# Table rows of eight words, sums cleared by ScalarE, edge attributes copied late, loads of x awaited one later: a graph network on one core

## The reference, cut to what matters

```python
def sage_layer(x, src, dst, Wl, bl, Wr):                  # three of them, relu after the first two
    agg = segment_sum(x[src], dst, 6250)
    cnt = segment_sum(ones, dst, 6250)
    return (agg / clip(cnt, 1)) @ Wl + bl + x @ Wr

x = layernorm(x + sage(x))
z = concatenate([x[dst], x[src], edge_attr_16])           # 100000 x 272
msg = sigmoid(z @ Wf.T + bf) * softplus(z @ Ws.T + bs)
h = relu(layernorm(batchnorm(segment_sum(msg, dst, 6250)) + x))
out = layernorm(x + (h + x))
```

## Time and profile before

| | us |
|---|---|
| median of 3 runs | 3432.28 (3430.3 to 3433.51) |
| the profiled execution | 3432.11 |
| its span | 3430.4 |
| PE busy / DVE / ACT / POOL | 2659.0 / 2137.3 / 1224.4 / 2346.7 |
| mean granted TensorE clock | 0.911 of full speed |

### The profile page before, as it was taken

The page is one execution under the profiler, slowest core; times in us unless marked ns, Lnnn a source line. Parts: engine busy times, 40 slices in busy tenths (PEclk is TensorE's granted clock), DMA queues, the critical chain, the costliest instruction groups (busy, mean ns, idle before and its releaser), DMA issues.

```text
span 3430.4 us, 69755 instructions
## 1 busy us (share of the span) xinstructions
PE 2659.0 (78%) x16221; PEld 1989.6 (58%) x16222; DVE 2137.3 (62%) x4942; ACT 1224.4 (36%) x1682; POOL 2346.7 (68%) x2399
## 2 busy tenths in 40 slices
PE   6578888675887875757888856688888888888874
PEld 6345555574655555645655556556666666666654
DVE  6635445466432224566544556778888888888886
ACT  2423333011000000110000002267888888888866
POOL 3667777576777777767777777467777777776610
PEclk8789999897999997878998978999999999999997
DMA  5354444323655562237777643344444444444411
GB/s 156 100 189 148 130 148 130 96 74 105 174 158 143 148 160 51 73 102 230 235 239 220 195 115 109 90 138 126 127 125 127 126 127 126 126 117 117 115 52 38
DMA packets 346021, 454.93 MB, mean 133 GB/s; under 512 B 135643, under 2 KB 260599, under 8 KB 342311
## 3 DMA queue, kind: packets, MB, share of 16 engines
q0 software_dynamic: 88624, 207.58, 22.5%
q10 hardware_dynamic: 127520, 197.33, 18.0%
q1 hardware_dynamic: 129768, 48.71, 5.8%
HBM read 357.03 MB, written 101.90 MB: 134 GB/s over the span
## 4 chain that ended last, share of the span: by engine, by line
POOL 35%; PE 20%; issue 20%; DVE 10%; DMA 9%; DVEq 2%; SPq 2%; ACT 2%; POOLq 0%; ACTq 0%
POOL shared L762 26%; POOL shared L802 9%; DMA shared<-q_dram,idx 6%; PE ps L957 6%; PE ps L948 4%; PE ps L1188 3%; PE ps L940 2%; SPq L637 1%; DVE work L2377 1%; DVE work L2060 1%; PE ps L967 1%; DMA dense_dram<-work 1%; ACT work L1521 1%; PE ps L1207 1%; PE ps L1191 1%
## 5 line engine op out<-in xcount | busy, mean ns | idle before, releaser
L762 POOL DMA_INDIRECT shared<-y_even,idx x1056 | 1039.4, 984 | 399.0 <-issue 311.5
L802 POOL DMA_INDIRECT shared<-q_dram,idx x784 | 779.1, 994 | 282.3 <-issue 224.5
L948 PE MATMUL ps<-shared,work 128*128 x4368 | 665.2, 301 | 324.4 <-SPq L598 194.2
L948 PEld LDWEIGHTS ps<-shared,work 128*128 128x128 f32 x4368 | 605.6, 211 | 400.0 <-issue 388.6
L2087 DVE TENSOR_TENSOR acc<-acc,ps 128x129 f32 x546 | 155.3, 284 | 848.3 <-PE ps L948 654.4
L762 POOL DMA_INDIRECT shared<-y_odd,idx x528 | 511.1, 968 | 178.1 <-issue 159.7
L1188 PE MATMUL ps<-pq,work 128*128 x1664 | 502.1, 404 | 142.6 <-issue 96.9
L2377 DVE TENSOR_TENSOR work<-ps,shared 128x256 f32<-128x256 f32 x832 | 294.5, 416 | 174.5 <-PE ps L1191 148.7
L1188 PEld LDWEIGHTS ps<-pq,work 128*128 128x128 f32 x1664 | 259.3, 196 | 237.8 <-issue 167.8
L967 PE MATMUL ps<-pq,work 128*128 128x385 bf16 x1456 | 296.1, 354 | 61.2 <-DVE work L2074 24.2
L1375 ACT CAST work<-ps 128x600 bf16<-128x600 f32 x260 | 159.6, 662 | 340.7 <-PE ps L940 314.8
(11 more groups left out here) (368 smaller groups left out, 3883.0 us busy)
## 6 DMA issues: line engine op xcount, KB each, us to landing
work<-counts_dram ACTq DMA_DIRECT2D x156, 384.0 KB
counts_dram<-work ACTq DMA_DIRECT2D x26, 1568.0 KB
ea_parts<-work ACTq DMA_DIRECT2D x128, 196.0 KB
ea_sb<-ea_parts SPq DMA_DIRECT2D x196, 128.0 KB
work<-counts_dram ACTq DMA_DIRECT2D x52, 416.0 KB
shared<-y_even,idx POOLq DMA_INDIRECT x1056
shared<-q_dram,idx POOLq DMA_INDIRECT x784
shared<-y_odd,idx POOLq DMA_INDIRECT x528
```

The lines of the kernel that those rows point to most:

```text
L762: pool.indirect_dma_start(msg[:, u, 0:F], None, y_two[layer % 2], bass.IndirectOffsetOnAxis(ap=idx[:, u:u + 1], axis=0)).then_inc(s_quad[q ...
L802: pool.indirect_dma_start(q_ring[:, u * 2 * F:(u + 1) * 2 * F], None, q_dram, bass.IndirectOffsetOnAxis(ap=idx[:, u:u + 1], axis=0)).then_ ...
L948: last = te.matmul(ps[:, SUM_BANKS[i], 0:FA], lhsT=oh4[:, OH_SLOTS[i], u, :], rhs=shared[:, bass.ds(place + u * FA, FA)], start=u == 0, st ...
```

## The change

- In all row loads of PE, DVE and SP's convolution loop the second load takes four words instead of three; the register arrays have eight entries. The table DMAs fill all eight words of a row.
- POOL's loop that clears `acc` goes; ACT clears a chunk after it has normalized it and issued the load of x, the last chunk after the last copy of q.
- The copy of the attributes is cut in its two halves, issued by SP ahead of the last two turns of layer 1; SP's last turn but one is taken out of the loop in all layers.
- ACT waits for a load of x before it issues the next one, and no longer right behind its issue.

```diff
             for at_, row_, first_, turns_, n_, wide_ in Q_TABLES:
-                from_dram = bass.AP(..., [[NIC * P, 1], [n_, turns_], [1, n_]])
+                from_dram = bass.AP(..., [[NIC * P, 1], [n_, turns_], [1, wide_ if turns_ > 1 else n_]])
...
-            def copy_sorted():
+            def copy_attributes(h):
                 with sp.If(unsorted < 1):
-                    for h in range(2):
-                        sp.dma_start(eaT_sorted[:, h * EP // 2:(h + 1) * EP // 2],
-                                     eaT[:, h * EP // 2:(h + 1) * EP // 2]).then_inc(s["ea_sorted"], 16)
+                    sp.dma_start(eaT_sorted[:, h * EP // 2:(h + 1) * EP // 2],
+                                 eaT[:, h * EP // 2:(h + 1) * EP // 2]).then_inc(s["ea_sorted"], 16)
...
                 turn(0)
-                if not layer:
-                    copy_sorted()
-                with sp.Fori(1, QG // RQ - 1) as it:
+                with sp.Fori(1, QG // RQ - 2) as it:
                     turn(it)
-                turn(QG // RQ - 1)
+                for h in range(2):
+                    if not layer:
+                        copy_attributes(h)
+                    turn(QG // RQ - 2 + h)
...
-                    sp.reg_load(n_regs[k:k + 4], q_regs[0:1, bass.ds(m * WIDE + (CONV_DONE_AT - WIDE + k), min(4, RC - k))])
+                    sp.reg_load(n_regs[k:k + 4], q_regs[0:1, bass.ds(m * WIDE + (CONV_DONE_AT - WIDE + k), 4)])
...
-            with pool.Fori(0, NCH) as it:
-                pool.wait_ge(s["var_z"], it + 1)
-                gp.tensor_copy(acc[:, bass.ds(it * (CW * FA), CW * FA)], zero[:, :].to_broadcast([P, CW * FA]))\
-                    .then_inc(s["acc_clear"], 1)
...
-                        pe.reg_load(t_regs[k:k + 4], q_regs[0:1, bass.ds(it * WIDE + (NEEDED_AT + k), min(4, IT - k))])
+                        pe.reg_load(t_regs[k:k + 4], q_regs[0:1, bass.ds(it * WIDE + (NEEDED_AT + k), 4)])
...
             def load_x(c):
+                if c:
+                    act.wait_ge(s["x_in"], c * 16)
+                alone(act)
                 act.dma_start(y_again[c % 2], xv[:, c * CW:(c + 1) * CW, :]).then_inc(s["x_in"], 16)
-                act.wait_ge(s["x_in"], (c + 1) * 16)
...
+            def clear_sums(it):
+                sc.copy(acc[:, it * (CW * FA):(it + 1) * (CW * FA)], zero[:, :].to_broadcast([P, CW * FA])).then_inc(s["acc_clear"], 1)
...
                 norm_x1(it)
                 if it < 2:
                     next_x(NCH - 2 + it)
+                if it < NCH - 1:
+                    clear_sums(it)
                 copy_x1(it)
                 copy_q(it)
+            clear_sums(NCH - 1)
...
-                    dve.reg_load(a_regs[k:k + 4], q_regs[0:1, bass.ds(it * WIDE + (SUMS_AT + k), min(4, IT - k))])
+                    dve.reg_load(a_regs[k:k + 4], q_regs[0:1, bass.ds(it * WIDE + (SUMS_AT + k), 4)])
```

More of the change, by code:

```diff
@@ L550, in _ @@
             for at_, row_, first_, turns_, n_, wide_ in Q_TABLES:
-                from_dram = bass.AP(q_regs_dram.tensor, q_regs_dram.offset + row_ * NIC * P + first_, [[NIC * P, 1], [n_, turns_], [1, n_]])
-                sp.dma_start(q_regs[0:1, at_:at_ + turns_ * wide_].rearrange("o (t e) -> o t e", e=wide_)[:, :, 0:n_] if turns_ > 1
+                from_dram = bass.AP(q_regs_dram.tensor, q_regs_dram.offset + row_ * NIC * P + first_, [[NIC * P, 1], [n_, turns_], [1, wide_ if turns_ > 1 else n_]])
+                sp.dma_start(q_regs[0:1, at_:at_ + turns_ * wide_].rearrange("o (t e) -> o t e", e=wide_) if turns_ > 1
                              else q_regs[0:1, at_:at_ + n_].rearrange("o (t e) -> o t e", e=n_), from_dram).then_inc(s["tab_back"], 16)
@@ L600, in turn @@
                 def turn(it):
-                    n = RQ if not isinstance(it, int) or it == 0 else RQ - AHEAD
+                    n = RQ if not isinstance(it, int) or it < QG // RQ - 1 else RQ - AHEAD
                     first = it * RQ + SUMMED_AT
@@ L629, in _ @@
             sp.wait_ge(s["p_done"], (NCH - 1) * 4 + 4)
-            n_regs = [sp.alloc_register(f"sp_n{q}") for q in range(RC)]
+            n_regs = [sp.alloc_register(f"sp_n{q}") for q in range(WIDE)]
             done_regs = [sp.alloc_register(f"sp_d{q}") for q in range(RC)]
@@ L909, in _ @@
             pe.wait_ge(s["tab_back"], TAB_Q)
-            t_regs = [pe.alloc_register(f"pe_t{u}") for u in range(IT)]
-            g_regs = [pe.alloc_register(f"pe_s{u}") for u in range(IT)]
+            t_regs = [pe.alloc_register(f"pe_t{u}") for u in range(WIDE)]
+            g_regs = [pe.alloc_register(f"pe_s{u}") for u in range(WIDE)]
             q_needed = [pe.alloc_register(f"pe_q{u}") for u in range(IT)]
-            d_regs = [pe.alloc_register(f"pe_d{u}") for u in range(IT)]
+            d_regs = [pe.alloc_register(f"pe_d{u}") for u in range(WIDE)]
             def sage_sums(layer):
@@ L924, in load_turn @@
                     for k in range(0, IT, 4):
-                        pe.reg_load(t_regs[k:k + 4], q_regs[0:1, bass.ds(it * WIDE + (NEEDED_AT + k), min(4, IT - k))])
-                        pe.reg_load(g_regs[k:k + 4], q_regs[0:1, bass.ds(it * WIDE + (PLACES_AT + k), min(4, IT - k))])
+                        pe.reg_load(t_regs[k:k + 4], q_regs[0:1, bass.ds(it * WIDE + (NEEDED_AT + k), 4)])
+                        pe.reg_load(g_regs[k:k + 4], q_regs[0:1, bass.ds(it * WIDE + (PLACES_AT + k), 4)])
                     for i in range(IT):
@@ L930, in load_turn @@
                             pe.reg_alu(q_needed[i], q_needed[i], layer * QG, ALU.add)
-                    return [pe.snap(r, min_val=0, max_val=(RQ - 1) * QT * FA) for r in g_regs]
+                    return [pe.snap(r, min_val=0, max_val=(RQ - 1) * QT * FA) for r in g_regs[0:IT]]
                 def count(n, k, slot):
@@ L972, in load_pairs @@
                     for k in range(0, IT, 4):
-                        pe.reg_load(d_regs[k:k + 4], q_regs[0:1, bass.ds(turn * WIDE + (PLACES_AT + TURNS * WIDE + k), min(4, IT - k))])
-                    return [pe.snap(r, min_val=0, max_val=(NGR - PT) * FA) for r in d_regs]
+                        pe.reg_load(d_regs[k:k + 4], q_regs[0:1, bass.ds(turn * WIDE + (PLACES_AT + TURNS * WIDE + k), 4)])
+                    return [pe.snap(r, min_val=0, max_val=(NGR - PT) * FA) for r in d_regs[0:IT]]
                 def pair_item(turn, i, place):
@@ L1969, in _ @@
             a3 = acc[:, :].rearrange("p (w f) -> p w f", f=FA)
[L1971 to L1974, removed]
+            a_regs = [dve.alloc_register(f"dve_a{i}") for i in range(WIDE)]
+            b_regs = [dve.alloc_register(f"dve_b{i}") for i in range(WIDE)]
+            f_regs = [dve.alloc_register(f"dve_f{i}") for i in range(WIDE)]
+            c_regs = [dve.alloc_register(f"dve_c{i}") for i in range(WIDE)]
             e_regs = [dve.alloc_register(f"dve_e{i}") for i in range(G)]
@@ L2029, in load_columns @@
                 for k in range(0, n, 4):
-                    dve.reg_load(c_regs[k:min(k + 4, n)], q_regs[0:1, bass.ds(first + k, min(4, n - k))])
+                    dve.reg_load(c_regs[k:k + 4] if n == IT else c_regs[0:n], q_regs[0:1, bass.ds(first + k, 4 if n == IT else n)])
                 return [dve.snap(r, min_val=0, max_val=(QL - 1) * QT) for r in c_regs[0:n]]
@@ L2078, in load_turn @@
                 for k in range(0, IT, 4):
-                    dve.reg_load(a_regs[k:k + 4], q_regs[0:1, bass.ds(it * WIDE + (SUMS_AT + k), min(4, IT - k))])
-                sums = [dve.snap(r, min_val=0, max_val=(NW - 1) * FA) for r in a_regs]
+                    dve.reg_load(a_regs[k:k + 4], q_regs[0:1, bass.ds(it * WIDE + (SUMS_AT + k), 4)])
+                sums = [dve.snap(r, min_val=0, max_val=(NW - 1) * FA) for r in a_regs[0:IT]]
                 return sums, load_columns(it * WIDE + COLS_AT, IT)
@@ L2106, in load_pairs @@
                 for k in range(0, IT, 4):
[L2107 to L2110, removed]
+                    dve.reg_load(b_regs[k:k + 4], q_regs[0:1, bass.ds(turn * WIDE + (SUMS_AT + TURNS * WIDE + k), 4)])
+                    dve.reg_load(f_regs[k:k + 4], q_regs[0:1, bass.ds(turn * WIDE + (PAIR_COLS_AT + k), 4)])
+                return ([dve.snap(r, min_val=0, max_val=(NW - 1) * FA) for r in b_regs[0:IT]],
+                        [dve.snap(r, min_val=0, max_val=(QL - 1) * QT) for r in f_regs[0:IT]])
             def add_pair(layer, turn, i, sums, columns):
```

4 lines of the change are left out of this document (2 added, 2 removed).

## The result

The changed kernel takes 3376.9 us in the median of four executions (3372.6 to 3383.4), the kernel before 3432.9 (3430.3 to 3433.5) on the same chip: ratio 0.984, 95% interval 0.9823 to 0.9857. That is 56 us less; forecast were 46 (3386), range 3370 to 3406. The profiled execution is the slowest of the four (3383.4, span 3381.6), 48.8 us of span less than the profiled one of before.

A forecast was written before the change was run, and what follows sets the result against it. No engine was full: PE paced layer 1's counting, POOL's gathers its end and layer 2, with layer 3's tail apart. 29.4 + 0.8 + 15 + 1 - 0.5 = 45.7, about 46 off 3432: 3386 us, range 3370 to 3406.

The forecast's parts named there:

- the 16.1 of PE's idle time: Layer 1's counting part: PE's idle time while the attributes are copied goes, 16.1 us gained.
- the +1 for the late copies: End of layer 1: the copies at their new place cost 1 us, bounds 0 and 25.
- the first rival: End of layer 1: copies paid in full where they land, 24 us more, 3410 us; chance 0.10.
- 11 + 2 + 1.3: Layer 1: four-word loads save 11 us in PE's counting gaps, 2 by the clock, 1.3 at the two tables' start.
- layer 1's 29.4 of forecast: Layer 1's whole gain: 16.1 + 11 + 2 + 1.3 - 1 = 29.4 us, under the 40 POOL has.
- Second rival: Layer 1's counting part: DVE's tiles or ACT's evictions take over the pace; without 13 us, 3399 us; chance 0.09.
- The rule of the Trainium skill on loads by register: All row loads, fifth rival: some 200 ns per register, four words 0.2 us longer than three; 3417 us, chance 0.01.
- x 5.8, loads 8.0, clears 4.4: Layer 3's tail: two waits for x 5.8 us, DVE's three-word loads 8.0, POOL's clears holding up a one-hot 4.4.
- a floor at 16.9: Layer 3's tail runs 16.9 us behind what its gathers allow, judged by layer 2's 8.8 us step; no more gain possible.
- The small terms: Start of layer 3: two DVE loads on the chain, 0.8 us; convolution: SP's shorter loads, 1 us, bounds 0 and 4.
- Rival 4: Clock stays up in the counting part, layer 1 gives its 40 us, the tail 16.9: 3374 us; chance 0.05.
- rival 3: End of layer 1: index loads stuck behind the copies stop POOL, 3446 us with 80 us a half; chance 0.03.

The follow-up runs named there:

- doubled: Changed kernel with each half of the attributes copied twice at the new place, the second time to another table: 3383.6 us, 0.9852 of the kernel before.
- the first execution: First profiled execution of the changed kernel, nothing else edited: 3383.4 us; median of its four executions 3376.9 us.
- the second execution: Profiled execution when the changed kernel was run once more, nothing edited: that run's median 3377.6 us, 0.9837 of the kernel before.
- no copy: Changed kernel without the copy of the attributes, which are read from the input directly: 3382.6 us, 0.9842 of the kernel before.
- the loads a turn ahead: Changed kernel with every second counting turn's registers loaded ahead on PE and DVE, into registers of their own: 3372.3 us, 0.9827 of the kernel before.

## Why the prediction was right

**The copy.** Forecast 15.1 less with its price: measured 15.4 alone and 15.9 taken back. Taking the 16.1 of PE's idle time and not the chain's 24.34 was the right choice; the +1 for the late copies was, if anything, too much. The 50 us by which indices lead were cover enough even for doubled copies. One mark was set wrongly: "PE waiting over 15 us in layer 1's last 60 us" was to show the first rival, but PE waited 15.7 for landed quads between 730 and 785 with no harm, and 18.0 in the last 60 us of the kernel that copies nothing: POOL is the bound in that stretch, and its stream never stopped.

**The loads in counting.** Forecast 11 + 2 + 1.3 = 14.3; by themselves they gave 17.5 at the layer's last gather. The mechanism is right: the long gaps went to the 1.8 us that was forecast, the short ones went altogether, and the start of the two tables gave 1.32 of 1.3. The size of the gaps is not: PE's waits fell by 14.9 with the loads alone and by 14.5 in the changed kernel, where 11 of 12 were taken. The earlier trace rows were misread there: 21.9 us less six long gaps of 2.69 leaves 5.8 for the six short ones, about 0.95 each and not 0.75, and nothing took their place. The clock was taken at 2; what is not wait came to 3.4 with the loads alone and to 1.7 and 3.5 in the changed kernel's two profiles, and a stretch at the lower level cost 1.0 us where 1.7 was taken.

So layer 1's 29.4 of forecast against 29.5 measured is in part luck. At PE's first sum of the two tables the first execution was 33.0 us ahead, and 3.5 of it was lost again up to the last gather, where the forecast had 1; in the second execution 35.0 became 34.3. Second rival: out; DVE's tile does end PE's gaps now, but at 1.8 us, as forecast from PE's own loads. The rule of the Trainium skill on loads by register ("Runtime: NRT & Kernel Launch", Instruction fetch mechanics) speaks of registers loaded from HBM, and these come from a table in SBUF; by it the time was to be 3417. Four words take 0.33 in both places of a line now, and that rival is out. So is the thought that the second load of a line is slow for its place.

**The tail.** Forecast: x 5.8, loads 8.0, clears 4.4, in all 18.2, of which 15 were taken, with a floor at 16.9. Singly they gave 6.9, 9.75 and 5.2, together 17.3 in the first execution and 18.8 in the second. So 15 was too cautious by 2.3 to 3.8, and the floor was none: it was taken from layer 2, where the last gather's DMA takes 4.73 us on the chain, and in layer 3 of the second execution it takes 3.80 and the whole step 6.87 instead of 8.8. A second thing failed in the working, the share of the engines: the 8.0 were counted as DVE's four loads "beside three on PE", but DVE's alone gave 3.4. ACT's clear of a chunk took 0.94 where 0.78 was worked out.

**The small terms.** The 0.8 at the start of layer 3 and the 1 in the convolution are not shown. POOL's stop of 2.41 us is gone in both profiles of the changed kernel, but from layer 1's last gather to layer 3's both took the kernel before's time to within 0.2 us; with the loads alone it was 1.6 less, and no run separates these. The convolution's 2.0 lie within its spread.

**The sum.** By the medians the four parts alone give 15.4 + 31.8 + 4.9 + 4.8 = 56.9, the whole 56: less than 1 us of overlap shows, though the tail's parts overlap by 3.0 to 4.6. The sum's mechanism held, and its sizes were low by 10 of 56. In the second execution, whose time lies at the median, layer 1 gave 4.9 more than forecast and the tail 3.8; in the first, layer 1's part of that was lost again. Rival 4 ("more is gained", 3374) was right in its number for the faster executions and in the tail; of its conditions the clock did not stay up in the counting part, and layer 1 gave 34.3 and not 40. Slower (rival 3): POOL waited for no index behind the copies, not even when they were doubled.

## What to carry to other kernels

Ask of a stall that a large transfer causes where in the program the same transfer meets an engine that has time, and measure the lead of what queues behind it; here some 50 us of lead left no price of 25 us of copies that could be told from the spread. Look at each form of a small instruction by its slowest kind: a load of three words cost more than one of four, and 0.4 us on the engine that paces, twice in each of its turns, was worth as much as the stall of 16 us (17.8 and 15.4 us by the medians). When several late things lie beside each other, price them together: two engines' loads gave 0.5 and 3.4 us singly and 9.75 as a pair.

## What was not expected of the hardware

The granted clock did not simply follow the length of PE's waits. From 225 us to the last count the three kernels that keep the copy at its old place, and so the stall ahead of that stretch, and load four words on PE read 1.00. The kernels that have no stall and the same loads read 0.98 and 0.99 (the changed kernel's two profiles), 0.99 (no copy) and 0.98 (doubled), with gaps of 1.8 us in all of them. In the changed kernel the clock fell to its lower level behind such a gap, the one of 1.81 us that ended at 418.25:

```profile
419.00:421.00 2.00, 2.00 (x11) 1.84 (x11) 0.99 (x4) 0.99 (x2) 1.60 (x2) 0.50 0.25 66
```

With the loads a turn ahead no gap is over 0.7 us and the clock reads 1.00 without a stall. So the gaps of 1.8 us go with what is left of the lower clock; why fewer of them have it behind them after a stall of 16 us was not tried.

Gathers of one shape take 0.94 us, or 1.0 to 1.5, in the same stretch, and which ones do differs between executions of one kernel: from POOL's last wait to the end of layer 1 it is 166.4 and 169.2 us in the two profiles of the changed kernel, a part of its spread that no edit here touches.
